# One plain product instead of two, with the raw products first and a result parked in DRAM

## What is computed

```python
# x: (32, 128, 2048); weight0: (2048, 2048); 8 adapters of rank 16; weight1: (16, 2048, 2048)
base  = einsum('bsi,oi->bso', x, weight0) + bias
delta = einsum('bsr,bor->bso', einsum('bsi,bri->bsr', x, a[id7]), b[id7])
x = x + base + scale[id7] * delta                 # stage 1 is the einsum with weight0
x = x + einsum('bij,bkj->bik', x, weight1[id14])  # stage 2
```

## Time and profile before

| | |
|---|---|
| median of 3 runs | 2579.33 us (2576.03 to 2581.75) |
| the profiled execution | 2576.68 us |
| its span (first to last instruction) | 2574.9 us |
| PE busy | 2557.1 us (99%) |
| DVE busy | 2114.2 us (82%) |
| POOL busy | 764.6 us (30%) |
| ACT busy | 1386.3 us (54%) |
| granted TensorE clock | 1.000 |

### The profile page before, as it was taken

One profiled execution on the slowest core, in us unless ns is written; L12 is line 12 of the kernel. 1 busy time (PEld: TensorE's weight loads), 2 busy tenths in 40 slices (PEclk: granted clock), 3 DMA queues, 4 the chain that ended last, 5 costly groups with the idle time before them and its releaser, 6 DMA issues.

```text
span 2574.9 us, 35471 instructions
## 1 busy us (share of the span) xinstructions
PE 2557.1 (99%) x12250; PEld 2114.8 (82%) x12250; DVE 2114.2 (82%) x1926; ACT 1386.3 (54%) x1478; POOL 764.6 (30%) x614
## 2 busy tenths in 40 slices
PE   8999999999999999999999999999999999999999
PEld 7888888888888888878888888888888888888887
DVE  6568999997888999898788787788877887887865
ACT  3324333334344333467676676766766666766755
POOL 5554332332333324220230231311311312212312
PEclk9999999999999999999999999999999999999999
DMA  9996642963576637878678677787899999998986
GB/s 357 352 379 197 203 135 99 290 213 131 162 239 216 168 131 242 308 264 280 243 258 297 240 263 279 247 278 260 290 355 355 353 349 365 353 324 320 312 325 228
DMA packets 213714, 686.19 MB, mean 266 GB/s; under 512 B 23424, under 2 KB 31776, under 8 KB 213536
## 3 DMA queue, kind: packets, MB, share of 16 engines
q1 hardware_dynamic: 204032, 649.33, 70.0%
q0 software_dynamic: 9216, 33.56, 6.7%
q10 hardware_dynamic: 288, 1.05, 0.1%
HBM read 650.29 MB, written 100.66 MB: 292 GB/s over the span
## 4 chain that ended last, share of the span: by engine, by line
PE 92%; DVE 4%; DMA 2%; issue 1%; ACT 0%; SPq 0%; POOL 0%; DVEq 0%; ACTq 0%; POOLq 0%
PE acc L1294 18%; PE acc L1295 18%; PE acc L1296 18%; PE acc L1211 12%; PE acc L1213 12%; PE acc L1212 12%; DVE tx L1165 1%; DVE ws L1165 1%; PE acc L1228 1%; PE acc L1250 1%; DMA bias_s<-bias 1%; DMA xb<-x_sums 1%; DMA xst<-xt 0%; DVE acc L1154 0%; DMA xb<-x 0%
## 5 line engine op out<-in xcount | busy, mean ns | idle before, releaser
L1165 DVE TENSOR_TENSOR ws<-wb,ws 128x1024 fp32r<-128x1024 f32 x968 | 1257.0, 1325 | 284.0 <-ACT ws L1001 268.2
L1001 ACT CAST ws<-wb 128x1024 fp32r<-128x1024 f32 x968 | 990.9, 1050 | 778.3 <-PE acc L1296 450.7
L1294 PE MATMUL acc<-ws,ops 128*128 128x512 f32 (+1 forms) x2048 | 799.9, 391 | 2.6 <-DVE ops L1165 2.3
L1295 PE MATMUL acc<-ws,ops 128*128 128x512 f32 (+1 forms) x2048 | 797.6, 389 | 0.0
L1296 PE MATMUL acc<-ws,ops 128*128 128x512 f32 (+1 forms) x2048 | 797.2, 389 | 0.0
L911 POOL TENSOR_TENSOR wb<-wb,eye_s 128x128 f32<-128x128 f32 x384 | 332.2, 897 | 1145.5 <-DMA wb<-w 1144.9
L1211 PE MATMUL acc<-tx,ws 128*128 128x512 f32 x1600 | 623.5, 390 | 4.5 <-DVE tx L1165 2.4
L1212 PE MATMUL acc<-tx,ws 128*128 128x512 f32 x1600 | 622.5, 389 | 0.0
L1213 PE MATMUL acc<-tx,ws 128*128 128x512 f32 x1600 | 622.5, 389 | 0.0
L1294 PEld LDWEIGHTS acc<-ws,ops 128*128 128x128 f32 x2048 | 384.6, 188 | 82.5 <-issue 6.2
L1296 PEld LDWEIGHTS acc<-ws,ops 128*128 128x128 f32 x2048 | 384.5, 188 | 81.0
(11 more groups left out here) (67 smaller groups left out, 1021.0 us busy)
## 6 DMA issues: line engine op xcount, KB each, us to landing
wb<-w SPq DMA_DIRECT2D x816, 512.0 KB, 6.8
xb<-x SPq DMA_DIRECT2D x78, 512.0 KB, 5.7
xb<-x POOLq DMA_DIRECT2D x64, 512.0 KB, 8.8
y<-acc SPq DMA_DIRECT2D x32, 1024.0 KB, 10.4
wb<-w_sums SPq DMA_DIRECT2D x64, 512.0 KB, 7.9
out<-ost SPq DMA_DIRECT2D x128, 256.0 KB, 7.4
xst<-xt SPq DMA_DIRECT2D x60, 512.0 KB, 6.4
ystage<-y SPq DMA_DIRECT2D x60, 512.0 KB, 7.3
```

The costliest lines, as they stand in the source:

```text
L1001: eng.copy(hi, src).then_inc(s_hi, 1)
L1165: eng.tensor_tensor(lo, src, hi, ALU.subtract).then_inc(s_lo, 1)
L1294: eng.matmul(dst, yh, wh, start=begin, stop=False)
L1295: eng.matmul(dst, yh, wl, start=False, stop=False)
```

## The change

1. The order of the products (`ORDER`) becomes (0,0), (0,1), (1,0), (1,1), then (0,2) ... (0,6), then (1,2) ... (1,6). The four products of raw weight blocks and raw x blocks are now products 0 to 3.
2. `PLAIN = (0,)`: the product (0,1) takes the form `Seven`. Stage 1 has 99 steps instead of 100.
3. The eight sets of outer weight sums move: four are due in the first product (`MADE_FIRST`) and four in the third, which is (1,0) in the form `Seven` (`MADE_THIRD`, from its start). None is due in the second.
4. The result of (1,0), called P, goes to slot 1 of `acc`, is stored to DRAM (`x_part`, four DMAs of 1 MB), and comes back into slot 2 (`part_back`, four DMAs of 1 MB, from the fifth step of (0,6) on, 11 us apart) before (1,3) uses it. Three of the four stores of X of group 0 are due 10 us later.
5. Waits for free slots are written with `STORES` and `FREE_BEHIND`; the banks of the small first matmuls are chosen by the new parity of the bank sets.

The diff, cut to its core:

```diff
+ORDER = [(0, 0), (0, 1), (1, 0), (1, 1)] + [(g, n) for g in range(NG) for n in range(2, K)]
+GRP, NUM = zip(*ORDER)
+POS = {gn: q for q, gn in enumerate(ORDER)}
-SLOT = ({"X": 0, "Y": 1, "Q": 2, "Z": 1}, {"X": 2, "Y": 1, "Q": 0, "Z": 1})
-TARGET = ("X", "Y", "Q", "X", "X", "Z", "X")
+SLOT = ({"X": 0, "Y": 1, "Q": 2, "Z": 1}, {"P": 1, "X": 2, "Y": 2, "Q": 0, "Z": 1})
+TARGET = (("X", "Y", "Q", "X", "X", "Z", "X"), ("P", "Y", "Q", "X", "X", "Z", "X"))
+STORES = {(0, "Y"): 1, (1, "P"): 2, (0, "Z"): 3, (1, "Z"): 4, (0, "X"): 1, (1, "Q"): 2, (1, "Y"): 1, (0, "Q"): 2, (1, "X"): 3}
+FREE_BEHIND = {(1, "P"): (0, "Y"), (0, "Q"): (1, "Y"), (1, "Q"): (0, "X"), (0, "Z"): (1, "P"), (1, "Z"): (0, "Z")}
...
-MADE_FROM = 10.0
-MADE_EVERY = 18.0
+MADE_FIRST = (10.0, 29.0, 48.0, 67.0)
+MADE_THIRD = (4.0, 21.0, 38.0, 55.0)
...
-PLAIN = (0, 1)
+PLAIN = (0,)
...
     def made_key(p):
-        return MADE_FROM + MADE_EVERY * p
+        return MADE_FIRST[p] if p < len(MADE_FIRST) else t_of(BEGIN[2]) + MADE_THIRD[p - len(MADE_FIRST)]
...
+                if (g, name) == (0, "X") and blk:
+                    key += 10.0
                 loads.append((key, "store", (g, name, blk)))
+    for blk in range(4):
+        loads.append((ev_key(last_step(POS[1, 0], blk), 3) + 6.0, "store", (1, "P", blk)))
+        loads.append((t_of(BEGIN[POS[0, 6]] + 4) + 11.0 * blk, "back", (blk,)))
...
+            def part_back(blk):
+                stored(eng, 0, "Q", blk)
+                stored(eng, 1, "P", blk)
+                eng.dma_start(acc[:, SLOT[1]["X"], blk, :], x_part[blk]).then_inc(s_back[blk], 16)
...
                     if k == 1 and opens:
-                        src = tile_view(SLOT[g]["X"], blk, ot)
-                        ev_done(eng, last_step(K * g, blk), ot)
+                        src = tile_view(SLOT[g][TARGET[g][0]], blk, ot)
+                        ev_done(eng, last_step(POS[g, 0], blk), ot)
                         if g:
-                            eng.wait_ge(s_y0[1][blk], 32)
+                            for p in (6, 7):
+                                for n in range(4):
+                                    made_kept(eng, p, n)
                     elif k == 3 and opens:
-                        ev_done(eng, last_step(K * g, blk), ot)
+                        if g:
+                            eng.wait_ge(s_back[blk], 16)
+                        else:
+                            ev_done(eng, last_step(POS[g, 0], blk), ot)
```

More of the change, by code:

```diff
@@ L35 @@
 LEAD = 13.0
+XS_AHEAD = 6.0
 X_ROLE = {"b11": (0, 0), "b12": (0, 1), "b21": (1, 0), "b22": (1, 1)}
@@ L90 @@
 BEGIN = [STEPS.index((q, 0)) for q in range(NG * K)]
-MADE = [(role, h) for role in FORM[2].w_need for h in range(2)]
+MADE = [(role, h) for role in FORM[POS[0, 2]].w_need for h in range(2)]
 def last_step(q, blk):
@@ L274, in program @@
     for q in range(NG * K):
-        n = q % K
+        n = NUM[q]
         for role in X_ROLE:
@@ L320, in program @@
     for q in range(NG * K):
-        n, s0 = q % K, BEGIN[q]
+        n, s0 = NUM[q], BEGIN[q]
         for role in ("a11", "a22"):
@@ L346, in program @@
     for g in range(NG):
-        q3 = K * g + 3
+        q3 = POS[g, 3]
         z_at = {0: (q3, 3), 1: (q3 + 1, 2), 3: (q3 + 1, 3), 2: (q3 + 1, 4)}
@@ L374, in program @@
             for ot in range(4):
-                (fast if q % K in (0, 2) and i in FORM[q].first else slow).append((ev_key(s, ot), s, ot))
+                (fast if NUM[q] in (0, 2) and i in FORM[q].first else slow).append((ev_key(s, ot), s, ot))
     fast.sort()
@@ L386, in program @@
             for blk in range(4):
[L387 removed]
+                key = ev_key(last_step(POS[g, n], blk), 3) + 1.2
                 if name == "Q":
@@ L475, in program @@
         bank = [ctx.enter_context(nc.psum_tensor(f"acc{i}", [P, 512], F32)) for i in range(8)]
-        acca = bank[7]
+        spare = 4 * (1 - SETS[0])
+        acca, order_at = bank[spare + 3], bank[spare + 2]
         s_ids = sem("s_ids")
@@ L492, in program @@
         s_mv = [[sem(f"s_mv{i}_{c}") for c in range(4)] for i in range(2)]
+        s_back = [sem(f"s_back{i}") for i in range(4)]
         s_y0 = [[sem(f"s_y0_{i}_{c}") for c in range(4)] for i in range(3)]
@@ L518, in program @@
                 k = XS[q][role]
-                if q % K in X_ADDED:
+                if NUM[q] in X_ADDED:
                     added[k] += 16
                     added_no[q, role] = added[k]
-                if q % K in X_SAVED:
+                if NUM[q] in X_SAVED:
                     kept[k] += 16
@@ L555, in ev_done, with stored, free_slot @@
             eng.wait_ge(s_copy if (s, ot) in by_copy else s_ev, ev_no[s, ot])
+        def stored(eng, g, name, blk):
+            eng.wait_ge(s_y0[SLOT[g][name]][blk], 16 * STORES[g, name])
+        def free_slot(eng, g, name, blk):
+            if (g, name) in FREE_BEHIND:
+                stored(eng, *FREE_BEHIND[g, name], blk)
         def blk_view(slot, blk):
@@ L675, in load_x @@
             def load_x(q, role, c):
-                g, n = q // K, q % K
+                g, n = ORDER[q]
                 slot = XS[q][role]
@@ L687, in load_x @@
                     i = X_PLAIN[n][1]
-                    m = K * g + 2 + i
+                    m = POS[g, 2 + i]
                     x_saved(eng, m, role, c)
@@ L695, in save_x @@
                 x_ready(eng, q, role, c)
-                eng.dma_start(x_sums[q // K, X_SAVED[q % K], k, j, c], x_tile(q, role, c))\
+                eng.dma_start(x_sums[GRP[q], X_SAVED[NUM[q]], k, j, c], x_tile(q, role, c))\
                     .then_inc(s_xv[XS[q][role]][c], 16)
             def load_w(q, role, h):
-                n = q % K
+                n = NUM[q]
                 if q:
@@ L707, in load_w @@
                 else:
-                    if q < K:
+                    if GRP[q] == 0:
                         made_kept(eng, MADE.index((role, h)), MADE_AS.index(what[1]))
@@ L728, in store_y0 @@
             def store_y0(g, name, blk):
-                slot, (big_o, big_j) = SLOT[g][name], HOME[name]
+                slot = SLOT[g][name]
+                if name == "P":
+                    for ot in range(4):
+                        ev_done(eng, last_step(POS[1, 0], blk), ot)
+                    eng.dma_start(x_part[blk], acc[:, slot, blk, :]).then_inc(s_y0[slot][blk], 16)
+                    return
+                big_o, big_j = HOME[name]
                 o, j = blk // 2, blk % 2
@@ L780, in _ @@
                     store_y0(*index)
+                elif kind == "back":
+                    part_back(*index)
                 elif kind == "raw":
@@ L811, in _ @@
                         y0_stored(0)
+                        y0_stored(1)
+                        for blk in range(4):
+                            stored(eng, 0, "Q", blk)
                     elif b == 0:
@@ L930, in _ @@
                     q, i = STEPS[s]
[L931 to L938, removed]
+                    (g, k), blk = ORDER[q], FORM[q].blk[i]
+                    name = TARGET[g][k]
+                    slot = SLOT[g][name]
+                    free_slot(eng, g, name, blk)
                     eng.wait_ge(s_mm, at["W", s, ot] + 1)
@@ L969, in _ @@
                         for blk in range(4):
-                            eng.wait_ge(s_y0[2][blk], 32)
+                            stored(eng, 1, "X", blk)
                     else:
@@ L1081, in _ @@
                     x, q, z = (blk_view(SLOT[g][name], blk)[:, :, cols] for name in ("X", "Q", "Z"))
-                    s = last_step(K * g + (3 if what == "z" else 4), blk)
+                    s = last_step(POS[g, 3 if what == "z" else 4], blk)
                     ev_done(eng, s, 2 * oh + 1)
@@ L1085, in _ @@
                         for ot in (2 * oh, 2 * oh + 1):
-                            ev_done(eng, last_step(K * g + 2, blk), ot)
-                        eng.wait_ge(s_y0[1][blk], 16 * (2 * g + 1))
+                            ev_done(eng, last_step(POS[g, 2], blk), ot)
+                        free_slot(eng, g, "Z", blk)
                         eng.tensor_tensor(z, x, q, ALU.add).then_inc(s_sum, 1)
@@ L1177, in _ @@
             for i in range(WARM):
-                eng.matmul(bank[0][:], tx[:, 0, 0, 0:P], tx[:, 0, 0, 0:512], start=True, stop=True)
+                eng.matmul(bank_at(0, 0)[:], tx[:, X_SLOT[0], 0, 0:P], tx[:, X_SLOT[0], 0, 0:512], start=True, stop=True)
             for blk in blocks:
@@ L1187, in _ @@
                         eng.wait_ge(s_key, 10)
-                        eng.matmul(bank[6][:, 0:NB], wide, put, start=True, stop=True).then_inc(s_put, 1)
+                        eng.matmul(order_at[:, 0:NB], wide, put, start=True, stop=True).then_inc(s_put, 1)
                     if blk == ("W", 1, 2):
```

24 lines of the change are left out of this document (12 added, 12 removed).

## The result

The changed kernel takes 2590.5 us (median of 4 runs, 2590.18 to 2591.89) against 2578.1 for the kernel before: a ratio of 1.0049, 95% interval 1.0037 to 1.0060. It is slower by 0.5%. The forecast was slower, 2586, with a range of 2569 to 2597.

A forecast was written before the change was run, and what follows sets the result against it. PE, busy 99% of the span, was taken as the bound. 2576.7 - 10.9 + 15.2 + 0.8 + 2 = 2583.8 us, or 2586 in the frame of the median; range 2569 to 2597.

The forecast's parts named there:

- One step less: Stage 1, seven steps instead of eight in one product: 48 matmuls fewer, -10.88 us of PE, called certain.
- Second product: (0,1) as Seven without made sums: no PE wait expected, 0 us, bounds 0 and 2.4.
- First product: (0,0) with four sets at later due times: its 1.2 us wait stays, change 0, bounds -1.2 and +1.2.
- Third product: (1,0) as Seven with 16 made sums: PE waits for DVE, +15.2 us, bounds 0 and 24.
- the turns: DVE and POOL alternate instructions on SBUF; each POOL sum costs DVE 2.2 us, with pairs 3.35 us apart.
- The count step by step: Third product followed per step from its start, DVE beside POOL's sums: PE's accumulated lateness reaches 15.2 us.
- New neighbours: (0,2) now follows (1,1): x sums wait for x tiles to be saved to DRAM, +0.8 us, bounds 0 and 1.5.
- The parked result: Start of (1,2): returning loads crowd full DMA queues ahead of an x save, +2 us, bounds 0 and 5.8.
- rival D: Start of (1,2): DMA crowding costs 6 us or more on top of A; 2592 to 2600 us, chance 0.08.
- B: Third product: a set slips into the fourth, 6 to 10 us of waits; 2577 to 2582 us, same, chance 0.25.
- C: Third product: made sums fit DVE's pauses and evictions, no step late; 2568 to 2572 us, faster, chance 0.23.
- A: The forecast: DVE and POOL alternating costs PE 13 to 20 us in the third product; 2584 to 2592, chance 0.44.

The follow-up runs named there:

- the cut sums: Changed kernel with the third product's 16 outer weight sums working on 16 of 1024 columns, waits and loads kept: 2576.05 us, ratio to before 0.9995.
- the fills: Changed kernel with the third product's 16 outer sums replaced by constant fills of the same tiles: 2576.5 us, ratio to before 0.9996.
- the cut bytes: Changed kernel with the four loads of the parked result cut to 16 of 2048 columns, at their old place: 2581.6 us, ratio to before 1.0013.
- the late return: Changed kernel with the parked result's four loads due in the second step of (1,2), 3 us apart: 2581.5 us, ratio to before 1.0017.

## Why the prediction was right, and where its sizes were off

- *One step less, -10.9.* Right: 4752 matmuls.
- *Second product, 0.* Right, 76.2 us with no wait.
- *First product, 0 (-1.2 to +1.2).* It lost 1.1 us less than before, since the later due times parted the two sets that ran back to back. Inside the bounds.
- *Third product, +15.2 (0 to 24).* Measured 14.5, shown to be the turns by the cut sums, and to be GpSimd's reading by the fills. The count step by step had PE late by 2.0, 5.7, 10.7, 13.3, 13.6 and 15.2 us; the starts show 0, 5.6, 8.3, 11.0, 13.3, 13.8 and 14.2, then 0.3 more. The second step wasn't late, since the third of DVE's instructions was done at 188.3 and the step was due at 188.7: DVE's evictions ended 2.1 us into the product, not 2.8, and the first split, at 179.88, began before POOL's set did and took 1.76 us. The bound by work that cannot go side by side (94 us) was near: 90.4 us by step starts. The exclusive lock of the Trainium skill (SBUF — State Buffer, section "Who interferes with whom"), taken by the letter at 3.53 us for a pair, would by an estimate have made it 18 to 19; the pairs again took 3.35.
- *New neighbours, +0.8.* Right in size for (0,2), 0.75. The reason given, DVE's wait for a save, is not what the traces show at the loss itself: the step that loses most (11.5 us, in (0,2) as in (1,2) before) is one in which DVE is full and a weight split takes 3.4 us beside an inner sum (at 373.29; 752.56 before). That the late x sums pushed this inner sum there is likely, but was not tried. At (0,6) 0.8 us came on top that I had at nothing; it stays in the kernel with the cut bytes and in that with the late return (the fourth step loses 1.5 us in each, 0.7 before), so it isn't the return of the result. The traces show where it lies: POOL issues two accumulations between the two inner sums of that step, the second sum begins at 689.62, 3.5 us after the first, and two x splits take 5.42 us beside it; before, the sums ran back to back and the splits took 4.58. No run tested that.
- *The parked result, +2 (0 to 5.8).* This term failed: about 9 us, outside its own bounds. I had read the right rows (the full queues and DVE's wait for a save in rows 9 and 10) but counted two 1 MB transfers ahead of one save. In fact load, accumulation and save of a tile follow one on the other and all three were slower, by 4.3, 1.5 and 5.8 us on the chain shown above; of these 11.6 us 2.6 came back, since the save was issued sooner after its accumulation. The reason for taking 2 of 5.8 was also a misreading: the row with a DMA share of 0.16 lies two steps after the start of (1,2), not half a step, and DVE is full in it (11.50 of 11.50 us). The price worked out for rival D, over 6 us, was the right size.
- *Rivals.* B (sets slip into the next product): did not happen, the last set ended at 262.4 us, 6 us before the end of the third product. C (the sums find DVE's pauses): ruled out by the cut sums. A and D came together. The median lies in A's own range (2583 to 2592), but the sum that gives it is D's: A's wait at its lower end and 9 us at the start of (1,2). So the direction was right for its stated main cause, the turns, and that the time came out within 5 us of the forecast is in part luck.
- *The frame.* The terms of the forecast add up to +7.1; the result is +12.4 against the median of before now known, 2578.1, and +13.2 by the spans. Of the 6.1 us missing by the spans 7 are the parked result and 0.8 is (0,6); the first product gave 1.1 back and the third 0.7; the rest is stage 2 and rounding.
- *The windows of rows 2.* The first product's window does not hold a whole product, as I had it: the product takes 90.8 us with its waits. No term of the sum hangs on it.

## What to carry to other kernels

Before a sum is given to GpSimd "for free", count DVE's instructions with two SBUF inputs in the same stretch: each GpSimd sum of 128x1024 that reads SBUF costs DVE 2.2 us here, and what is too much comes out on PE if DVE feeds it. Place such sums where DVE is idle or works from PSUM; moving two of the four sets out of the third product brought back 9 us that the change had lost. And when a result is parked in DRAM, bring it back where no chain of load, accumulate and save is running: issuing four loads of 1 MB 10 to 42 us later was worth 9 us.

## What the runs showed of the hardware

The granted clock fell to its lower level (1.2 GHz) during or just after waits of PE. In the changed kernel a wait of 4.38 us is followed by matmuls that start 0.42 to 0.43 us apart instead of 0.23:

```profile
205.17 0.77 PE L1249 MATMUL acc<-tx,ws 128*128 128x512 f32 x1 [4.38 <-DVE tx L1203]
205.74 0.63 PE L1250 MATMUL acc<-tx,ws 128*128 128x512 f32 x1
206.16 0.63 PE L1251 MATMUL acc<-tx,ws 128*128 128x512 f32 x1
```

There are three such stretches, of 6.8, 3.4 and 3.4 us. PE still waited for DVE at the end of each step that holds one, so DVE set the pace there and PE only waited less. For the second stretch a pair of windows shows it, the fifth step of the third product, first in the changed kernel, then in the one with the cut bytes, whose execution had no such stretch there:

```profile
232.10:245.30 13.20, 12.74 (x48) 10.06 (x48) 13.20 (x4) 5.94 (x9) 11.85 (x4) 0.87 1.03 415
...
232.10:245.30 13.20, 11.15 (x48) 8.93 (x48) 13.17 (x5) 7.54 (x11) 11.94 (x4) 1.00 1.03 416
```

At a clock of 0.87 PE is busy for 12.74 us of the step, at 1.00 for 11.15, and the step is 13.2 us long in both. The other two have no such pair among the runs. A PE that is "busy" longer at a lower clock is therefore no sign of a loss by itself.
